# The last batches of a two-layer recurrent and attention kernel: output group 28 two steps earlier, its gated product three steps later

## The chip, the cores and the metric

One core of a Trainium2 chip. The metric is the device time of one execution in microseconds. The kernel before takes 791.45 us (median of three runs, 791.45 to 791.87).

## The reference, cut to what matters

The input x is 16 batches of 256 tokens by 256 features, f32. Layer 0 is a diagonal complex recurrence beside a gated MLP; the change doesn't touch it. Layer 1 is this:

```
xn = layernorm(x)
q = xn @ Wq                      # 16 heads of 192, 64 of them rotated
c_kv, k_rope = split(xn @ Wkv_a) # latents of 64, one shared rotated key of 64
k, v = from rmsnorm(c_kv) @ Wkv_b
scores = q . k / sqrt(192), causal
out = softmax(scores) @ v @ Wo   # 256 x 256 for each batch
g = silu(x @ base_w + b + 2 * lora(top 2 of 8 experts))
x = x + out * g
```

## The kernel before, in words

The key and value weights are folded into the query and output weights ahead of the loop, so that scores and values work on the latents of 64. Every f32 product of projections is done as three fp32r matmuls (high by high, high by low, low by high; helper `three`, line 549).

Layer 1 is a loop over steps n, written out on each engine in the same order; an engine works through its own list and waits for the others on semaphores. Ten steps make a batch: step n computes the scores of unit n. A unit is some rows and heads of a batch, of kind M, W or T. The last batch, 15, has units 150 to 159, by `LAST_ORDER` the W units (whole-width ones) last: 156 to 159.

What happens to a unit n: TensorE makes its scores in step n (`l1_s`, lines 747 to 773), at the earliest when the mask step of unit n-1 has been done and ahead of anything queued later; VectorE adds the mask and takes the row extremes in step n (`most`, line 1589); ScalarE takes the exponentials (`exps`, n+1); VectorE inverts the sums (`inverse`, n+2); GpSimd multiplies (`normalise`, n+2); VectorE turns the weights into PT (`turn_weights`, n+4, before the mask step of n+4 or, in every tenth step, behind it). Two banks take the scores in turn.

What happens to a batch: TensorE multiplies the turned weights by the latents (`l1_pv`, line 795: the value products); the sums lie in four banks. ScalarE copies one half of them to `oh` (`latents`, line 1078, high part), VectorE subtracts this for the low part `ol` (`latents_low`, line 1653). Half k%2 of batch k//2 is output group k: 24 matmuls on TensorE (`l1_out(k)`), then on VectorE the product with the gate (`gated_out(k)`, line 1664, writes `fo[k % 2]`), on GpSimd the addition of x (`residual(k)`, line 2113), and SyncE stores the result. For the last batch the value products come in two pieces: the first at step 160 (needs the turned weights of units 150 to 155), the last at step 162 (needs all ten and the reads of the first piece).

At which step these things stand in each engine's list is set for the last two batches by the table `LAST` (line 178): V the value products, L the reads by ScalarE and VectorE, O the output groups, R the gated product, C the residual; each row has batch 14, then batch 15, and in each the first and second half. Batch 14's two output groups are 28 and 29, those of batch 15 are 30 and 31. In a step of TensorE the order is: value products, scores, output group. In a step of VectorE it is: `latents_low`, `gated_out`, `inverse`, `turn_weights`, `most`. In a step of ScalarE: `latents`, `exps` of the unit before.

Six of the eight banks are a ring (`ring`) that value sums, output groups and others share. `shared_bank_order` (line 142) lists the uses in the order of the steps, use number i has bank `ring[i % 6]`, and `free_shared` makes TensorE wait until the use six places earlier has been read, which for an output group is its gated product:

```
place = jplace[(kind, i)]
if place >= RING:
    for name, value in freed_by(*jorder[place - RING]):
        w.wait_ge(name, value)
...
return {"o": [("ob", i + 1)], ...
```

Of the kernel before, what the change touches and what calls it, by code (L numbers as in the profile page):

```python
# [141 lines left out]
def shared_bank_order():  # L142
# [34 lines left out]

LAST = {
    "V": ((154, 154), (160, 162)),
    "L": ((158, 159), (163, 166)),  # L180
    "O": ((159, 161), (165, 167)),
    "R": ((161, 165), (166, 171)),
    "C": ((164, 165), (168, 173)),
}
LAG = {"V": (LAG_V, LAG_V), "L": (LAG_L, LAG_L), "O": LAG_O, "R": LAG_R, "C": LAG_C}
STEPS = max(LAST["C"][1]) + 1
# [2071 lines left out]
```

How the kernel before makes its waits and increments, by code:

```python
    def wait_ge(self, name, value):  # L99
        if value > self.reached.get(name, 0):
            self.e.wait_ge(self.sems[name], value)
            self.reached[name] = value
# [287 lines left out]
        def after_weights(w):  # L390
            w.wait_ge("wo_t", 4)
            w.wait_ge("wml", 1)
            w.wait_ge("wmh", 1)
# [1 line left out]
        def after_first(w):  # L395
            w.wait_ge("wo_t", 2)
# [1 line left out]
        def after_up(w):  # L398
            w.wait_ge("f1", 8 * NC)
# [1 line left out]
        def after_mlp(w):  # L401
            w.wait_ge("f1", 8 * NC)
            w.wait_ge("f2", 16 * NC)
            w.wait_ge("hsl", 8 * NC)
            w.wait_ge("hsh", 8 * NC)
            w.wait_ge("bu", NC)
# [1 line left out]
        def after_l0(w):  # L408
            after_mlp(w)
            w.wait_ge("xo", 2 * NC)
            w.wait_ge("th0", 2 * NC)
            w.wait_ge("dx", 2 * NC)
            w.wait_ge("ty", 2)
# [1 line left out]
        def qt_free(w, n):  # L415
            if n == 0:
                after_up(w)
            elif n < 3:
                after_mlp(w)
            else:
                w.wait_ge("s", UNITS * ((n - 3) // 2) + HALF_DONE[(n - 3) % 2])
# [10 lines left out]
        def place(e, w, b, h, heads=range(4)):  # L433
            n = 2 * b + h
            w.wait_ge("qq", g_nth[2 * n + 1])
            qt_free(w, n)
            for i in heads:
                for j in range(2):
# [7 lines left out]
        @block.sync  # L447
# [26 lines left out]
                load_x(c)  # L474
            w.wait_ge("w1h", 4)
            w.wait_ge("w1l", 4)
# [22 lines left out]
            def spread(b):  # L500
                w.wait_ge("kvw", b + 1)
                if b == 0:
                    after_mlp(w)
```

## Time and profile before

| | us |
|---|---|
| median of the runs | 791.45 |
| profiled execution | 791.67 |
| its span, first to last instruction | 789.9 |
| TensorE busy | 778.6 |
| VectorE busy | 681.7 |
| ScalarE busy | 524.5 |
| GpSimd busy | 479.5 |

PE is TensorE, DVE VectorE, ACT ScalarE, POOL GpSimd. Times of rows are from the start of the span. A line number in a row is that of the code, and for a matmul of a projection always that of the helper `three`. A row of a timeline can merge several instructions (x2, x24), and its length is then that of all of them. Batch 15's unit 155 is masked by VectorE just before 765.1, 156 in the step that begins at 765.13, and 158 at 770.24. Output group 28 is the run of 24 matmuls that begins at 769.76. The median time from the issue of a store of `fo` to its landing is 2.0 us.

### The profile page before, as it was taken

The page shows a single profiled execution, that of the slowest core. Times are in us where ns is not written, and L with a number is a line of the kernel's source. Part 1 is how long each engine was busy: PE and PEld are TensorE (multiplying, and loading weights), DVE is VectorE, ACT ScalarE, POOL GpSimd, SP SyncE. Part 2 cuts the span into 40 slices and gives each one's busy share as a digit, 9 for nine tenths or more (in the row PEclk, how much of TensorE's full clock was granted, in tenths as well). Part 3 has the DMA queues.
Part 4 walks back from the last instruction along what each step waited for, and adds up shares of the span by engine and source line. Part 5 has one row for each costly group of instructions (what it writes and reads, how often), then busy time and mean ns, then how long its engine had stood idle before and what let it go on. Part 6 is the DMA issues. An engine that isn't in the chain of part 4 may idle for free.

```text
span 789.9 us, 23152 instructions
## 1 busy us (share of the span) xinstructions
PE 778.6 (99%) x7976; PEld 711.5 (90%) x7976; DVE 681.7 (86%) x2616; ACT 524.5 (66%) x1612; POOL 479.5 (61%) x1278
## 2 busy tenths in 40 slices
PE   9999999999999999999999999999999999999988
PEld 7889889888889889898998989899898998989867
DVE  6998897888688899989898998989989898998885
ACT  5554454445555787777767777677777867777682
POOL 6880202202236696776867768686776867768673
PEclk9999999999999999999999999999999999999999
DMA  8600220000002222322222322223222222322220
GB/s 302 253 2 2 62 82 27 1 1 1 1 15 52 40 46 52 61 54 36 48 46 50 64 39 50 40 46 55 56 55 35 48 46 49 63 39 53 34 52 28
DMA packets 101334, 41.15 MB, mean 52 GB/s; under 512 B 91744, under 2 KB 98400, under 8 KB 100576
## 3 DMA queue, kind: packets, MB, share of 16 engines
q1 hardware_dynamic: 98896, 38.89, 22.1%
q8 instruction: 63, 1.03, 0.5%
q10 hardware_dynamic: 2320, 0.79, 0.4%
q14 instruction: 55, 0.45, 0.2%
HBM read 14.47 MB, written 4.19 MB: 24 GB/s over the span
## 4 chain that ended last, share of the span: by engine, by line
PE 92%; DVE 4%; ACT 1%; POOL 1%; issue 1%; ACTq 0%; POOLq 0%; DVEq 0%
PE bank L549 63%; PE bank L773 11%; PE bank L795 8%; PE bank L766 3%; PE bank L629 2%; PE bank L815 1%; PE bank L566 1%; DVE SM L1608 1%; PE bank L681 1%; ACT SM L1065 1%; DVE PT L1631 1%; PE bank L641 1%; PE bank L655 1%; POOL SM L2051 1%; PE bank L700 0%
## 5 line engine op out<-in xcount | busy, mean ns | idle before, releaser
L1065 ACT ACTIVATE SM<-SM,stb 128x224 f32<-128x224 f32 (+7 forms) x512 | 207.2, 407 | 62.7 <-DVE stb L1608 58.2
L2051 POOL TENSOR_SCALAR SM<-SM,stb 128x224 f32<-128x224 f32 (+7 forms) x512 | 195.2, 396 | 67.5 <-DVE stb L1615 66.1
L549 PE MATMUL bank<-yh,wq_lo 128*128 128x256 f32 x512 | 150.6, 294 | 0.0
L549 PE MATMUL bank<-yh,wq_hi 128*128 128x256 f32 x512 | 144.7, 283 | 0.0
L549 PE MATMUL bank<-yl,wq_hi 128*128 128x256 f32 x512 | 144.6, 282 | 0.0
L773 PE MATMUL bank<-KT,QT 128*128 128x192 f32 (+4 forms) x640 | 120.9, 327 | 1.7 <-DVE stb L1608 1.7
L1608 DVE CUSTOM_DVE_ANT_0 SM<-bank,CONST 128x224 f32<-128x224 f32 (+3 forms) x320 | 97.2, 348 | 23.3 <-PE bank L773 20.9
L1631 DVE STREAM_TRANSPOSE PT<-SM 128x128 f32<-128x128 f32 (+2 forms) x232 | 99.7, 462 | 16.7 <-PE bank L795 16.7
L773 PEld LDWEIGHTS bank<-KT,QT 128*128 128x128 f32 x640 | 97.5, 190 | 5.3 <-DVE stb L1608 3.6
L549 PEld LDWEIGHTS bank<-yh,wq_lo 128*128 128x128 f32 x512 | 97.1, 190 | 1.4
L549 PEld LDWEIGHTS bank<-yh,wq_hi 128*128 128x128 f32 x512 | 97.1, 190 | 0.0
L549 PEld LDWEIGHTS bank<-yl,wq_hi 128*128 128x128 f32 x512 | 97.0, 189 | 0.0
L1065 ACT ACTIVATION_READ_ACCUMULATOR SM<-SM,stb 128x1 f32 x512 | 96.9, 189 | 0.0
L950 ACT ACTIVATE hs<-bank,B 128x512 f32<-128x512 f32 x64 | 44.0, 688 | 75.3 <-PE bank L549 70.2
L2044 POOL TENSOR_TENSOR QA<-QA 128x256 f32<-128x256 f32 x62 | 45.9, 740 | 58.7 <-DVE QA L1579 58.7
L1037 ACT ACTIVATE QT<-bank 64x512 f32<-64x512 f32 x128 | 75.6, 590 | 6.5 <-PE bank L549 5.0
L1579 DVE TENSOR_TENSOR QA<-bank,TR 128x512 f32<-128x512 f32 x124 | 79.4, 683 | 0.1
L549 PE MATMUL bank<-woe_hi,ol 128*128 128x256 f32 x256 | 75.4, 294 | 0.7 <-issue 0.7
L549 PE MATMUL bank<-w2h,hl 128*128 128x256 f32 x256 | 74.0, 289 | 0.2 <-DVE w2l L1352 0.2
L549 PE MATMUL bank<-w2h,hh 128*128 128x256 f32 x256 | 72.4, 283 | 0.0
L549 PE MATMUL bank<-w2l,hh 128*128 128x256 f32 x256 | 72.3, 283 | 0.0
L549 PE MATMUL bank<-woe_hi,oh 128*128 128x256 f32 x256 | 72.1, 281 | 0.0
(229 smaller groups left out, 2068.9 us busy)
## 6 DMA issues: line engine op xcount, KB each, us to landing
QT<-QA SPq DMA_DIRECT2D x240, 64.0 KB, 2.1
PT<-KV SPq DMA_DIRECT2D x256, 16.0 KB, 1.8
out<-fo SPq DMA_DIRECT2D x32, 128.0 KB, 2.0
X<-in_x SPq DMA_DIRECT2D x7, 512.0 KB, 11.5
stage<-in_wqn SPq DMA_DIRECT2D x2, 1024.0 KB, 5.3
stage<-in_wo SPq DMA_DIRECT2D x2, 1024.0 KB, 4.9
stage<-in_w1t SPq DMA_DIRECT2D x4, 256.0 KB, 5.0
stage<-in_w2t SPq DMA_DIRECT2D x2, 512.0 KB, 6.2
```

The lines of the kernel that those rows point to most:

```text
L549: i = e.matmul(dst, a, b, start=(first and j == 0), stop=(last and j == 2), skip_group_check=skip)
L766: j = e.matmul(sbank[n % 2][32 * i:32 * i + 32, at:to], KT[b % 3][:, p, 32 * kb:32 * kb + 32], Q[:, :, kb:3, i, :], start=True, stop=True)
L773: j = e.matmul(sbank[n % 2][:, at], Q[:, q, :, :].rearrange("p h c -> p (h c)"), KT[b % 3][:, p, 0:32 * q + 32], start=True, stop=True)
L795: j = e.matmul(sums[64 * half:64 * half + 64, :, 32 * q:32 * end], C[rows_, kb // 2, at], PT[rows_, 2 * half:2 * half + 2, kb, q:end, :], ...
L950: e.activation(hs[g % 2][:, :], fbank[g % 2][:, :], ACT.Gelu, bias=B1[:, g % 8:g % 8 + 1]).then_inc(SEM["gelu"], 1)
L1037: i = e.activation(QT[r, (2 * b + g // 2) % 3, p, :, g % 2:4:2, :].rearrange("p n j c -> p j n c"), src[r, :, :, :], ACT.Copy)
L1065: i = e.activation(M[:, at], M[:, at], ACT.Exp, bias=S[:, 0, j:j + 1], scale=-1.0, accum_out=S[:, 1, j:j + 1])
L1579: i = e.tensor_tensor(A[:, part, :, :, g % 2, :], src, TR[:, part, :].rearrange("p (n c) -> p n c", n=8).unsqueeze(1).broadcast_to([128, 2 ...
L1608: i = e.tensor_tensor_reduce(M[:, at], bk[:, at], mask[:, 224 - 32 * q:256], 1.0, 3e38, ALU.add, ALU.min, S[:, 0, j:j + 1])
L1631: return e.transpose(PT[:, slot, 0:k, q:q + some, :].rearrange("p k q c -> p q k c"), src)
L2044: e.tensor_tensor(A[:, 0, 0, :, :], A[:, 0, 0, :, :], A[:, 1, 1, :, :], ALU.subtract)
L2051: i = e.tensor_scalar(P[:, at], P[:, at], S[:, 2, j:j + 1], 1.0, ALU.mult, ALU.mult)
```

## The change

Four rows of the table `LAST` get other steps for batch 14. ScalarE and VectorE read the first half of its sums in step 156 instead of 158. Output group 28 is issued in step 157, behind the scores of unit 157, instead of in step 159 behind those of unit 159. Its gated product is in VectorE's step 164 instead of 161, which is behind the turn of unit 159 (step 163). The residuals of groups 28 and 29, and with them their stores, stand one step later each.

```diff
 LAST = {
     "V": ((154, 154), (160, 162)),
-    "L": ((158, 159), (163, 166)),
-    "O": ((159, 161), (165, 167)),
-    "R": ((161, 165), (166, 171)),
-    "C": ((164, 165), (168, 173)),
+    "L": ((156, 159), (163, 166)),
+    "O": ((157, 161), (165, 167)),
+    "R": ((164, 165), (166, 171)),
+    "C": ((165, 166), (168, 173)),
 }
```

## Rows read from the trace of the kernel before

**Rows 1.** The page, part 4: share of the span on the chain, by engine.
```profile
PE 92%; DVE 4%; ACT 1%; POOL 1%; issue 1%; ACTq 0%; POOLq 0%; DVEq 0%
```

**Rows 2.** Busy time of each engine in three stretches of the tail, us from the start.
```profile
762.50:770.00 7.50, 5.45 (x38) 3.81 (x26) 6.98 (x40) 6.91 (x31) 4.80 (x16) 1.00 0.18 50
770.00:775.60 5.60, 5.48 (x121) 4.71 (x121) 5.46 (x21) 2.90 (x10) 3.21 (x8) 1.00 0.00 0
775.60:789.90 14.30, 10.81 (x200) 10.40 (x200) 4.92 (x9) 2.18 (x4) 3.13 (x5) 0.97 0.12 39
```

**Rows 3.** The chain that ended last, from 772 us: start, length in us.
```profile
772.14 0.77 DVE PT L1631 x2
...
772.96 2.60 PE bank L795 x92
775.56 3.04 PE bank L549 x24
778.60 1.92 PE bank L795 x117
```

**Rows 4.** Timeline of VectorE: start, length in us, idle before in brackets.
```profile
765.13 0.19 DVE L1615 RECIPROCAL stb<-stb 128x6 f32<-128x6 f32 x1
...
768.37 1.29 DVE L1653 TENSOR_TENSOR ol<-bank,oh 128x512 fp32r<-128x512 f32 x2 [0.46 <-ACT oh L1078]
769.57 0.16 DVE L1615 RECIPROCAL stb<-stb 128x2 f32<-128x2 f32 x1
...
770.24 0.36 DVE L1608 CUSTOM_DVE_ANT_0 SM<-bank,CONST 128x224 f32<-128x224 f32 x1
...
773.52 0.70 DVE L1631 STREAM_TRANSPOSE PT<-SM 128x512 f32<-128x512 f32 x1
774.14 0.40 DVE L1664 SCALAR_TENSOR_TENSOR fo<-bank,PT 128x256 f32<-128x256 f32 x1
...
774.76 1.28 DVE L1631 STREAM_TRANSPOSE PT<-SM 128x512 f32<-128x512 f32 x2
776.31 1.29 DVE L1653 TENSOR_TENSOR ol<-bank,oh 128x512 fp32r<-128x512 f32 x2 [0.27 <-ACT oh L1078]
777.52 0.70 DVE L1631 STREAM_TRANSPOSE PT<-SM 128x512 f32<-128x512 f32 x1
```

**Rows 5.** Timeline of ScalarE, the same columns.
```profile
764.91 0.19 ACT L1065 ACTIVATION_READ_ACCUMULATOR SM<-SM,stb 128x1 f32 x1
...
767.74 1.09 ACT L1078 ACTIVATE oh<-bank 128x512 fp32r<-128x512 f32 x2
...
773.57 0.49 ACT L1065 ACTIVATE SM<-SM,stb 128x224 f32<-128x224 f32 x1 [1.50 <-DVE stb L1608]
...
775.61 1.09 ACT L1078 ACTIVATE oh<-bank 128x512 fp32r<-128x512 f32 x2 [0.96 <-PE bank L795]
```

**Rows 6.** Timeline of TensorE, the same columns.
```profile
762.58 1.90 PE L773 MATMUL bank<-KT,QT 128*128 128x128 f32 x10
765.13 1.08 PE L773 MATMUL bank<-KT,QT 128*128 128x224 f32 x4 [0.65 <-DVE stb L1608]
766.66 1.08 PE L773 MATMUL bank<-KT,QT 128*128 128x224 f32 x4 [0.46 <-DVE stb L1608]
...
769.76 0.36 PE L549 MATMUL bank<-woe_hi,ol 128*128 128x256 f32 x1 [0.71 <-issue]
```

**Rows 7.** Timeline of GpSimd, the same columns.
```profile
763.81 4.62 POOL L2051 TENSOR_SCALAR SM<-SM,stb 128x32 f32<-128x32 f32 x15 [1.66 <-DVE stb L1615]
...
775.81 0.74 POOL L2113 TENSOR_TENSOR fo<-fo,X 128x256 f32<-128x256 f32 x1
```

**Rows 8.** Busy times and granted clock after TensorE's last matmul.
```profile
786.40:788.00 1.60, 0.01 (x1) 0.00 (x0) 0.42 (x1) 0.00 (x0) 0.72 (x1) 1.00 0.00 0
788.00:789.00 1.00, 0.00 (x0) 0.00 (x0) 0.00 (x0) 0.00 (x0) 0.00 (x0) 0.97 0.38 130
789.00:789.90 0.90, 0.00 (x0) 0.00 (x0) 0.00 (x0) 0.00 (x0) 0.00 (x0) 0.50 0.01 1
```

## The prediction

> **What bounds the kernel now.** First the chain that ended last, by engine: TensorE holds 92% of it, VectorE 4% [rows 1]. Over the whole span the kernel is TensorE's, but the change touches only the last 30 us or so, and those have to be read by themselves. The busy times in three stretches show it [rows 2]: from 762.5 to 770.0 us TensorE is busy for 5.45 of 7.50 us and VectorE for 6.98; from 770.0 to 775.6 both are nearly full; from 775.6 on TensorE leads with 10.81 us of work and VectorE has 4.92. The chain, followed through the hand-over, says where the lead changes [rows 3]: VectorE's last turn of a non-W unit (unit 155) ends at 772.91, TensorE's first value products of batch 15 start at 772.96, then come without a pause output group 29 (775.56, 3.04 us) and the last value products (778.60). So everything up to 772.9 is set by VectorE, and everything behind it by TensorE's queue. The profiled execution took 791.67 us, 0.22 above the median of 791.45; its span is 789.9 and the 1.77 us around it are taken as they are.
>
> **What is moved, step by step.** No instruction is added or removed. I write O28 for output group 28, and G28 for its gated product.
>
> 1. *Reads of batch 14's first half, step 158 to 156 (ScalarE and VectorE).* In their old place they cost VectorE a wait of 0.46 us for ScalarE and 1.29 us of work, starting 0.63 us after ScalarE's copy [rows 4, 5]: VectorE was through with step 157 at 768.37 - 0.46 = 767.91. In the new place ScalarE can start them only when the exponentials of unit 154 are out, about 765.11, since they stand behind these in its queue; the first step of VectorE behind unit 155 starts 0.63 later, at 765.74, instead of 765.13. The sums that they read were complete long before (TensorE began the next unit's scores at 762.58 [rows 6]). The two subtractions end at 767.03, and the next instruction, which before began 1.20 after the first subtraction (769.57 - 768.37), starts at 766.94. Steps 156 and 157 then take VectorE 2.78 us as before (765.13 to 767.91), to 769.72.
> 2. *O28, step 159 to 157 (TensorE).* TensorE began it 0.10 us after the subtractions (769.66 to 769.76), so now at 767.13, behind the scores of unit 157, which still start at 765.13 and take 1.08 [rows 6]. It takes 3.04 us, the length of its twin O29 in the chain [rows 3]. Now the scores of units 158 and 159 are queued behind it. Those of 158 run from 770.17 to 771.25 instead of from 766.66. VectorE, free at 769.72, has a reciprocal and a turn to do first, 0.67 us by the old distance from 769.57 to 770.24, and would take these scores at 770.4: it waits until 771.29, 0.04 behind their end. That is 1.05 us later than the old 770.24 [rows 4]. The scores of 159 follow directly and are done by about 772.3, before VectorE asks for them at 773.9. GpSimd is no limit: its multiplications run at 4.62 us for 15 [rows 7], the six of unit 154 would be done about 769.1, and they are wanted at 769.7.
> 3. *Up to the first value products.* From the mask step of 158 VectorE runs as before: second half's subtractions, reciprocal, turn of 155. The end of that turn, and with it the start of the value products, comes 1.05 later: 774.01 instead of 772.96. So the 2.05 us in which TensorE idled in the first stretch [rows 2] are only partly filled and partly moved behind the scores of 159.
> 4. *G28, VectorE's step 161 to 164, and what waits for it.* This is the step that decides. The shared banks are a ring of six, handed out in the order that `shared_bank_order` writes. Counting it out, O28 is place 308, then one pad, four banks for batch 15's sums, and O29 is place 314: six further, the same bank. `free_shared` therefore makes TensorE wait, ahead of O29 and of all that is queued behind it, for G28. Before, G28 ended at 774.54 and O29 could start at 775.56, so the wait cost nothing. The move puts G28 behind the subtractions of group 30 (step 163) and behind the turn of unit 159 in VectorE's queue. The subtractions of group 30 need the first value products complete. The chain becomes: value products 774.01 to 776.61 (2.60); ScalarE's copies 0.05 later; VectorE's subtractions 0.70 after these start, as before (775.61 to 776.31), at 777.36; the last turn 1.21 further (776.31 to 777.52), at 778.57; G28 another 0.62 further (as 773.52 to 774.14 behind such a turn) at 779.19, 0.40 long [rows 4, 5]; O29 0.10 behind it, at 779.69. Before it was at 775.56. TensorE stands still from 776.61 to 779.69, 3.1 us, where it had none.
> 5. *Who would have hidden it.* O29 was the cover for VectorE's tail: its 3.04 us ran beside the subtractions and the last turn, which ended at 778.22, just before the last value products at 778.60. Now O29 comes after that tail, and the tail's wait is in the open. The last value products themselves find their operands ready. The turns of 157 and 158 are no nearer limit: exponentials of 159 shift by 1.05 with the mask step, from 773.57 to 774.62, and release the turns 1.19 later (774.76 before), at 775.8; 1.28 us of turns end at 777.1, before 777.36 [rows 4, 5].
> 6. *The residual and the store of 28.* They follow G28, some 5 us later than before. G30, in the same output buffer, waits for that store; G28 ends at 779.6, 0.74 us of GpSimd [rows 7] and some 2 us of transfer bring it to about 782.5, and G30 can't come before O30, which stands behind O29 and the last value products, is done (about 787). Nothing. Steps 165 and 166 of the copies on GpSimd hold up nothing either: its multiplications end with step 161. SyncE's queue holds at that time only the stores.
>
> The sum: +1.05 (VectorE's wait for the scores of 158) and +3.1 (O29 behind G28) is 4.15 us; everything behind O29 keeps its order and lengths. 791.67 + 4.15 = 795.8 for the profiled execution, 795.6 on the median's footing.
>
> Bounds of what the trace doesn't show. The wait of O29 has no row. From below it would be nothing or a gain, if VectorE reached G28 before 776; from above it is the 3.1 us and a TensorE that runs slower after them. I take 3.1, since each of its parts is the distance between two rows of this tail. The shift of 1.05 lies between -0.46 (only ScalarE's old wait gone) and 3.04 (VectorE held for the whole of O28); I take 1.05, since it comes from the starts of both engines' next work, and both have rows.
>
> The clock: the granted clock is 1.00 in the first two stretches, and the third's 0.97 comes from its very end [rows 2]. After TensorE's last matmul (786.4) it is 1.00 to 788, 0.97 in the next microsecond and 0.50 at the end [rows 8], so it fell to the lower of its levels (1.2 GHz for 2.4) after some 2.5 us without work. The pause in front of O29 would be 3.1 us.
> The Trainium skill ("TensorE: Matmul & The Clock Gate", section "Why this matters for your kernels") warns of just such pauses between bursts of matmuls, since idleness puts the array back to half rate; by that rule O29 would run at the lower level at least in part, while by the sum above it doesn't. The page and these rows speak the same way, so this is a rival with a real chance.
>
> **The rivals.**
>
> *A. The clock falls in the new pause.* For it: it fell after about 2.5 us at the end. Against it: that was one fall, and in the first stretch TensorE idled for 2.05 of 7.50 us in pieces without one. O29's 3.04 us would take up to 3.04 us more if all of it ran at 0.50; the clock should rise again on the way, so I take half, 1.5: 797.1.
>
> *B. Faster: the holes are filled and nothing new opens.* The place is O29's start. If G28 is through before 776 (another bank for O29, or VectorE early), O29 follows the value products directly; with TensorE's 2.05 us of idle time of the first stretch all gained, 789.4. It decides by whether VectorE's queue or TensorE's brings O29's bank. Against it: the ring's count, and that G28 stands behind the subtractions which themselves need the value products.
>
> *C. Only the ring's wait.* VectorE isn't held up by the scores of 158 (O28 shorter or the queue less strict than I have it), only step 4 costs: 3.1, 794.6.
>
> *D. No effect.* The wait exists, but TensorE's other work covers it: 791.5. Against it: only the last value products are left behind it, and they are queued after O29.
>
> **The numbers.** Forecast 0.50, A 0.33, C 0.10, D 0.03, B 0.04. The likeliest is 795.6, its own range 795.0 to 796.3. For 8 in 10 the range takes in A with half of its scatter and most of C: 794.0 to 798.0; B, D and a full loss of the clock are outside. A change of 0.2% (1.6 us) either way is about what a measurement here can tell from no change. Slower by more than that: forecast, A and C, 0.93; same 0.03; faster 0.04.
>
> **What would show it.** Step 2: O28 starts near 767.1, behind the scores of 157, and VectorE waits some 0.9 us for the scores of 158. Step 3: value products start near 774.0. Step 4: a pause of TensorE of 3 us in front of O29, released by VectorE's G28. Step 5: the last value products follow O29 at once. A: granted clock below 1 in the rows of 779 to 783, O29 longer than 3.04. I am wrong if O29 starts before G28, if there is no such pause, or if the value products start before 773.

## The result and the profile after

The changed kernel takes 797.54 us (median of five runs, 797.25 to 798.42), the kernel before 791.45 in the same comparison: a ratio of 1.0077 (95% interval 1.0066 to 1.0088), 6.1 us slower. The profiled execution took 798.28 us with a span of 796.4.

The code up to the tail is the same, but the time that it takes is not: over all profiles of this study the mark that I measure tails from, the start of the scores of unit 155 (the first row of [rows 6]), lies between 762.08 and 763.26. From there on the profiles of one kernel repeat: e3_early and e10_early_look are the same program, and the way from the mark to the end of the span is 28.17 and 28.16 us. Before, the mark is at 762.58 and the span ends 27.32 us later; here it is at 762.46, and the end comes 33.94 us later. The tail is 6.62 us longer.

The chain that ended last, after (answers to [rows 3]):

```profile
772.96 0.68 DVE PT L1631 x2
...
773.68 2.63 PE bank L795 x92
...
776.34 0.61 ACT oh L1078
...
777.07 0.43 DVE ol L1653
...
778.36 0.62 DVE PT L1631
778.97 0.32 DVE fo L1664
...
779.34 5.49 PE bank L549 x24
784.82 2.26 PE bank L795 x121
787.09 3.06 PE bank L549 x24
```

Read it downwards. VectorE turns unit 155, the first value products run, ScalarE copies their sums, VectorE subtracts, turns unit 159 and then makes the gated product of group 28 (`fo`); only when that is out does TensorE start group 29, at 779.34. Before, the third piece of this chain was already group 29, straight behind the value products. And group 29 now takes 5.49 us where it took 3.04, the last value products 2.26 where they took 1.92.

TensorE's timeline (answers to [rows 6]):

```profile
762.46 1.90 PE L773 MATMUL bank<-KT,QT 128*128 128x128 f32 x10
765.00 1.08 PE L773 MATMUL bank<-KT,QT 128*128 128x224 f32 x4 [0.64 <-DVE stb L1608]
767.01 0.36 PE L549 MATMUL bank<-woe_hi,ol 128*128 128x256 f32 x1 [0.93 <-ACT oh L1078]
...
769.94 1.78 PE L773 MATMUL bank<-KT,QT 128*128 128x224 f32 x8
773.68 2.61 PE L795 MATMUL bank<-PT 32*64 32x384 f32 x96 [1.97 <-DVE PT L1631]
779.34 0.58 PE L549 MATMUL bank<-woe_hi,ol 128*128 128x256 f32 x1 [3.05 <-DVE fo L1664]
```

Group 28 is now the run from 767.01. The scores of 158 and 159 (769.94, eight matmuls) come behind it. Two pauses stand in brackets: 1.97 us ahead of the value products, 3.05 us ahead of group 29.

VectorE's timeline (answers to [rows 4]):

```profile
765.62 1.29 DVE L1653 TENSOR_TENSOR ol<-bank,oh 128x512 fp32r<-128x512 f32 x2 [0.67 <-ACT oh L1078]
...
770.95 0.39 DVE L1608 CUSTOM_DVE_ANT_0 SM<-bank,CONST 128x224 f32<-128x224 f32 x1 [0.68 <-PE bank L773]
...
777.07 1.29 DVE L1653 TENSOR_TENSOR ol<-bank,oh 128x512 fp32r<-128x512 f32 x2 [0.30 <-ACT oh L1078]
778.27 0.70 DVE L1631 STREAM_TRANSPOSE PT<-SM 128x512 f32<-128x512 f32 x1
778.90 0.39 DVE L1664 SCALAR_TENSOR_TENSOR fo<-bank,PT 128x256 f32<-128x256 f32 x1
```

The subtractions of group 28 wait 0.67 us for ScalarE, the mask step of 158 waits 0.68 us for the scores that stand behind group 28, and the gated product follows the last turn at once.

Busy times and granted clock around the long pause (TensorE's busy time is the first figure behind the length, the granted clock the third from the end):

```profile
777.00:778.00 1.00, 0.00 (x0) 0.00 (x0) 0.93 (x2) 0.42 (x1) 0.00 (x0) 1.00 0.00 0
778.00:779.00 1.00, 0.00 (x0) 0.00 (x0) 1.00 (x3) 0.00 (x0) 0.00 (x0) 0.83 0.00 0
779.00:780.00 1.00, 0.66 (x3) 0.67 (x4) 0.28 (x1) 0.00 (x0) 0.63 (x1) 0.50 0.00 0
...
785.00:786.00 1.00, 1.00 (x61) 1.00 (x58) 0.29 (x1) 0.00 (x0) 0.63 (x1) 0.76 0.00 0
```

The clock goes from 1.00 to 0.50 in the microsecond from 778, while TensorE still waits, and is back in the microsecond from 785. At 0.50 a matmul of group 29 starts every 0.213 us instead of every 0.119.

From the mark, the value products start 11.22 us later against 10.38 before: 0.84. The pause adds 3.05. The slow clock adds 2.45 (5.49 - 3.04) and 0.34 (2.26 - 1.92). Together 6.7, against the 6.62 measured.

### The profile page after: what moved, and what is told of

It is laid out like the page before. It is cut to its first block, busy times and chain, and to the rows that moved or that the text cites. A ratio compares the mean times of both kernels' runs of the same rounds, so it can differ in the third digit from the quotient of the medians.

```text
span 796.4 us, 23151 instructions
## 1 busy us (share of the span) xinstructions
PE 780.8 (98%) x7976; PEld 714.2 (90%) x7976; DVE 681.1 (86%) x2616; ACT 522.9 (66%) x1612; POOL 478.7 (60%) x1278
## 4 chain that ended last, share of the span: by engine, by line
PE 92%; DVE 3%; ACT 1%; POOL 1%; issue 1%; ACTq 0%; POOLq 0%; DVEq 0%
PE bank L549 63%; PE bank L773 11%; PE bank L795 8%; PE bank L766 3%; PE bank L629 2%; PE bank L815 1%; PE bank L566 1%; DVE SM L1608 1%; PE bank L681 1%; ACT SM L1065 1%; DVE PT L1631 1%; PE bank L641 1%; PE bank L655 1%; POOL SM L2051 1%; PE bank L700 0%
## 5 line engine op out<-in xcount | busy, mean ns | idle before, releaser
L549 PE MATMUL bank<-woe_lo,oh 128*128 128x256 f32 x256 | 73.0, 285 | 0.0
```

The lines of the kernel that those rows point to most:

```text
L549: i = e.matmul(dst, a, b, start=(first and j == 0), stop=(last and j == 2), skip_group_check=skip)
```

## The experiments

The kernel before ran beside the experiments, in four groups with medians of 791.64, 791.61, 791.53 and 791.58 us, and in none of those 67 runs was the mean granted clock below 0.999. Tails are counted from the mark as above, minus the 27.32 us of before.

**Another bank for group 29 (e1_banks).** In the changed kernel:

```diff
+    i, j = js.index(("o", 2 * NB - 3)), js.index(("o", 2 * NB - 2))
+    js[i], js[j] = js[j], js[i]
     return js
```

> The changed kernel, with the ring places of output groups 29 and 30 exchanged, so that group 29 has a bank that nobody has to free and group 30 gets the bank of group 28. Theory (the bank's wait and the clock that falls in its pause make nearly all of the loss): the pause of 3.05 us before group 29 is gone, the granted clock stays 1.00 to the end of the matmuls, value products still start about 0.8 us late, so about 792.2 us. Rival 1 (the late gated product costs by itself, on VectorE or by the late store): at least 795 us although group 29 starts on time. Rival 2 (the clock falls because of the other holes, before the value products): clock still at 0.50 somewhere behind 774 us, about 794 to 795 us. Rival 3 (B of the prediction, the filled holes are a gain): 789.4 us.

Median 793.25 us (8 runs), ratio 1.0021 (1.0011 to 1.0031), tail +0.82. Its chain around group 29:

```profile
774.47 2.61 PE bank L797 x92
777.08 3.05 PE bank L551 x24
780.12 1.92 PE bank L797 x118
```

Group 29 starts the moment the value products end (774.47 + 2.61 = 777.08) and takes 3.05. With the late gated product still in step 164, nearly all of the loss has gone: its lateness costs nothing by itself, what costs is that it holds the bank. The median is 1 us above what I expected. Part of that is the clock, as the runs of e3_early show below; but the five runs at full clock, too, have a median of 793.12. The profiled one of them (793.20) is late before the tail begins: its mark is at 763.26, 0.68 us behind that of the kernel before. What makes that time differ is not shown.

**Only the gated product late (e2_product).** In the kernel before:

```diff
-    "R": ((161, 165), (166, 171)),
-    "C": ((164, 165), (168, 173)),
+    "R": ((164, 165), (166, 171)),
+    "C": ((165, 166), (168, 173)),
```

> The kernel before with only the gated product of group 28 moved from step 161 to 164 and the residuals of 28 and 29 to 165 and 166; reads and output group 28 stay in steps 158 and 159. Theory: group 29 waits for its bank for about 3.05 us, the clock falls in that pause and costs 1.7 to 2.8 us more, value products start on time at about 773.0: 796.2 to 797.3 us. Rival (it takes both halves of the change, because group 28's early place makes the holes in which the clock falls): the wait only, clock 1.00, 794.5 us. Rival 1 of the first run would give the same loss with group 29 on time.

Median 797.02 us, ratio 1.007 (1.0056 to 1.0084); all five runs have a mean clock of 0.995 to 0.998. In its profile the tail is +4.55: a pause of 3.05 us, and group 29 at 4.54 us. This half of the change alone makes 5.4 of the 6.1 us, the clock's part included.

**Only the reads and group 28 early (e3_early).** In the kernel before:

```diff
-    "L": ((158, 159), (163, 166)),
-    "O": ((159, 161), (165, 167)),
+    "L": ((156, 159), (163, 166)),
+    "O": ((157, 161), (165, 167)),
```

> The kernel before with only the reads of batch 14's first half moved to step 156 and output group 28 to 157; gated product and residuals stay where they were. Theory: VectorE waits about 0.7 us for ScalarE and 0.7 us for the scores of unit 158, in place of its old 0.46 us, value products start about 0.8 us late, no wait for the bank, clock 1.00: 792.2 us, the same as e1_banks within 0.3. Rival 3 (filled holes are a gain): 789.4 to 790 us. Rival (the shift is caught up later): 791.5 us.

Median 793.21 us (9 runs), ratio 1.0021 (1.0011 to 1.0031); tail +0.85 in the profile, with a clock of 1.00 from the mark to the last matmul. So moving group 28 into TensorE's idle time is a loss of 0.85 us, not a gain: VectorE gets the scores of 158 late. The runs are in two groups. Five, with a mean clock of 0.999 or more, took 792.47 to 793.21 us; four, with 0.997 or 0.998, took 793.85 to 795.22. e1_banks has the same two groups, five at 792.37 to 793.31 and three at 793.97 to 794.99. The median of e3_early's five is 792.49, 0.85 us above the kernel before, as in the tail.

**The long pause filled (e4_filled).** In the changed kernel, 18 matmuls ahead of group 29's wait, whose sums are overwritten:

```diff
+                        if 2 * d + qt == 2 * NB - 3:
+                            w.wait_ge("oth", evacuated(d, 1))
+                            w.wait_ge("otl", evacuated(d, 1))
+                            w.wait_ge("ob", 2 * NB - 5)
+                            for c in range(6):
+                                three(jof("o", 2 * NB - 2)[:, 0:256], oh[1][:, c % 8, :], ol[1][:, c % 8, :],
+                                      woe_hi[:, c % 8, :], woe_lo[:, c % 8, :], True, True)
                         l1_out(2 * d + qt)
```

> The changed kernel, with 18 further matmuls of group 29's own kind (128x256, 0.12 us each, 2.2 us in all; their sums are overwritten later and reach no result) on TensorE in the pause before group 29; the wait for the bank stays. Theory (two costs that stand in a row, wait and clock): the clock stays 1.00, group 29 still starts when the gated product is done and takes 3.04 us: 795.2 us, that is 2.3 us less than the changed kernel. Rival (the matmuls of group 29 are slow for another reason, as sharing memory with VectorE or the store): group 29 still takes about 5.5 us and the time stays at 797.5 us.

```profile
774.13 2.63 PE bank L795 x92
...
779.42 0.32 DVE fo L1671
...
779.78 3.15 PE bank L549 x24
```

```profile
779.78 0.39 PE L549 MATMUL bank<-woe_hi,ol 128*128 128x256 f32 x1 [0.72 <-DVE fo L1671]
```

```profile
779.00:780.00 1.00, 0.28 (x2) 0.22 (x2) 0.73 (x2) 0.00 (x0) 0.19 (x1) 1.00 0.00 0
```

The added matmuls leave 0.72 us of the pause idle, and the granted clock stays 1.00. Group 29 still waits for the gated product (779.42 to 779.74) and then takes 3.15 us instead of 5.49. The tail is +3.98 us, beside the 4.15 of my sum, which left the clock out. So wait and clock are two costs in a row, and the slow matmuls were the clock's doing. The median is 796.59 (ratio 1.0063, 1.005 to 1.0075), 1.4 above what I expected. Two of the five runs have a mean clock of 0.998 (797.05 and 797.61). Neither has a profile; the 1.97 us pause ahead of the value products, which is not filled here, may be the cause, but that is not shown. The three at 0.999 or more took 796.00 to 796.59, so the clock is not all of it: in the profiled one (796.00) the mark is 0.32 us later than before, and the rest is open.

**The gated product in step 163 (e5_step163).** In the changed kernel, ahead of the last turn:

```diff
-    "R": ((164, 165), (166, 171)),
+    "R": ((163, 165), (166, 171)),
```

> The changed kernel with the gated product of group 28 one step earlier on VectorE: step 163, behind the subtractions of group 30, ahead of the turn of unit 159. Theory (pause plus clock): the product starts 0.62 us earlier and group 29 with it, the pause is 2.4 us instead of 3.05. If the clock falls by then as it did in the changed kernel (some 2.3 us into the pause), it falls here too and the time is 0.6 us below that of the changed kernel; if this pause is short enough for the clock to stay, 2.3 to 3.3 us below, about 794.6 us. Rival (only a place behind all of VectorE's turns costs): as e3_early, 792.5 us.

```profile
774.00 2.63 PE bank L795 x92
...
778.67 0.34 DVE fo L1664
...
779.05 4.62 PE bank L549 x24
```

```profile
779.05 0.42 PE L549 MATMUL bank<-woe_hi,ol 128*128 128x256 f32 x1 [2.45 <-DVE fo L1664]
```

The pause is 2.45 us, 0.60 shorter, and the clock falls all the same, after group 29 has begun (0.63 in the microsecond from 779, then 0.50): 4.62 us. Its tail is +4.80, beside +5.45 in the second profile of the changed kernel (the next run). The median is 797.63 (ratio 1.0071, 1.0058 to 1.0083), not told from the changed kernel's: from run to run these times differ by more than the 0.6 us that the shorter wait gives back.

**The changed kernel once more (e7_again).**

> The changed kernel itself once more, beside the others on the same chip, for a second profile of its pause. Theory: pause 3.05 us, clock at 0.50 somewhere from 778 us on, cost of the clock between 1.5 and 2.8 us from run to run, median near 797.5 us. Rival (the fallen clock of the first profile was a rare event): clock 1.00, near 795.6 us.

Median 797.07 us (796.96 to 799.37), ratio 1.0074 (1.0061 to 1.0086). The two pieces of its chain and its clock:

```profile
779.40 4.54 PE bank L549 x24
783.94 1.98 PE bank L795 x119
```

```profile
779.00:780.00 1.00, 0.60 (x5) 0.60 (x6) 0.35 (x2) 0.00 (x0) 0.57 (x1) 1.00 0.00 0
780.00:781.00 1.00, 1.00 (x10) 1.00 (x9) 0.00 (x0) 0.00 (x0) 0.16 (x1) 0.81 0.00 0
783.00:784.00 1.00, 1.00 (x13) 0.78 (x20) 0.02 (x1) 0.00 (x0) 0.00 (x0) 0.50 0.00 0
784.00:785.00 1.00, 1.00 (x74) 1.00 (x81) 0.40 (x1) 0.00 (x0) 0.52 (x1) 0.99 0.00 0
```

The same pause, but the clock falls 1.2 us or so after TensorE has resumed, and it is back at about 784. Here it costs 1.50 and 0.06 us where the first profile had 2.45 and 0.34. All ten runs of the changed kernel had a mean clock of 0.995 to 0.998.

**The shorter pause: filled, and profiled again (e8_hole_filled, e10_early_look, e11_early_look).** e8 is e3_early with 12 matmuls ahead of the value products, whose sums are overwritten; the other two are e3_early unchanged, one run each:

```diff
+                if n == 160:
+                    w.wait_ge("ob", 2 * NB - 5)
+                    for c in range(4):
+                        three(jof("o", 2 * NB - 2)[:, 0:256], oh[0][:, c, :], ol[0][:, c, :],
+                              woe_hi[:, c, :], woe_lo[:, c, :], True, True)
```

> e3_early with 12 further matmuls (1.45 us, their sums reach no result) on TensorE behind the scores of unit 159, in the pause of 1.97 us before the first value products. The runs of e3_early and e1_banks lie in two groups: those whose mean granted clock is 0.999 to 1.0 at 792.4 to 793.3 us, those with 0.997 or 0.998 at 793.9 to 795.2. Theory (in those the clock fell in or behind this shorter pause): with the pause filled all runs keep 0.999 or more, and the median is 792.5 us with no run above 793.4. Rival (the scatter comes from another place): medians and scatter as e3_early, 793.2 us, some runs at 0.997.

> e3_early once more for a profile. Theory: if this run is one of those with a mean clock below 0.999 (4 of 9 had it), its rows show a granted clock of 0.50 that begins at or behind the pause before the first value products, some 772 to 776 us, and the time is 1.4 to 2.7 us longer; else it is as e3_early's profile. Rival: the clock falls somewhere else, or is 1.00 in a long run.

> As e10_early_look, for a further chance to see one of the runs with the lower mean clock; the same expectations.

e8: median 792.45 us, 11 runs from 792.25 to 793.07, every clock 0.999 or 1.0; ratio 1.0012 (1.0003 to 1.0021). The upper group is gone, though in the profile 0.54 us of the pause stays idle. e8 ran on another chip than e3_early, e10 and e11 on the same chip as e8. e10 had a clock of 1.00 and took 792.75 us. e11 was one of the others (mean 0.998, 793.57 us):

```profile
773.31 3.74 PE bank L795 x96
777.05 3.44 PE bank L549 x24
```

```profile
772.00:773.00 1.00, 0.00 (x0) 0.00 (x0) 1.00 (x4) 0.41 (x2) 0.32 (x1) 1.00 0.00 0
773.00:774.00 1.00, 0.69 (x16) 0.42 (x24) 1.00 (x7) 0.08 (x1) 0.59 (x2) 1.00 0.00 0
774.00:775.00 1.00, 1.00 (x32) 0.69 (x24) 0.88 (x2) 0.99 (x4) 0.91 (x2) 0.73 0.00 0
775.00:776.00 1.00, 1.00 (x32) 0.86 (x24) 0.98 (x3) 0.00 (x0) 0.72 (x2) 0.50 0.00 0
...
777.00:778.00 1.00, 1.00 (x9) 1.00 (x6) 0.20 (x1) 0.90 (x2) 0.00 (x0) 0.56 0.28 92
```

The pause of 1.97 us ends at 773.31; the clock falls in the microsecond from 774, with TensorE busy again, and is back in the one from 777. The value products take 3.74 us instead of 2.60 and group 29 3.44 instead of 3.05: 1.5 us.

**VectorE unloaded (e6_weigh, e9_unloaded, e12_ahead).** If VectorE bounds all up to the first value products [rows 2, 3], what nobody waits for should leave that stretch. e6 moves the gate's product of batch 15 from step 154 to 165:

```diff
-                if n and (d := sum_of(n - 1)) is not None:
+                if n and (d := sum_of(n - 1)) is not None and d < NB - 1:
                     weigh(d)
+                if n == 165:
+                    weigh(NB - 1)
```

> The kernel before with one thing moved that the change left where it is: the product of the gate of batch 15 (VectorE, 0.58 us on the chain at step 154, not wanted until group 30's gated product in step 166) goes to step 165, where VectorE has an idle time of 2.2 us. Theory (up to 772.96 us VectorE is the bound and TensorE behind it): the first value products start 0.4 to 0.6 us earlier and all behind them follows, about 0.5 us less than before. Rival (TensorE's value products of batch 14 or ScalarE's exponentials hold that stretch): no change within 0.1 us.

Median 791.64 us beside 791.61, ratio 0.9998 (0.9989 to 1.0007): no difference told. In its profile the value products start 0.33 us earlier from the mark, and the tail is -0.31. That is about half of the 0.58 us that left, because the rival is in part right: VectorE now waits 0.33 us at 762.61 for TensorE's value products of batch 14, where before it waited for nothing. The rest is lost in the scatter of the times.

e9 has this edit of e6 and moves more:

```diff
-LAST_LORA, LAST_SUM, LAST_SPREAD = 152, 153, 149
+LAST_LORA, LAST_SUM, LAST_SPREAD = 152, 161, 149
+    i = js.index(("o", 2 * NB - 4))
+    js[i], js[i + 1] = ("pad", i), js[i]
-    "R": ((161, 165), (166, 171)),
-    "C": ((164, 165), (168, 173)),
+    "R": ((164, 165), (166, 171)),
+    "C": ((165, 166), (168, 173)),
```

> The kernel before with VectorE's work that nobody waits for taken out of its bound stretch: the sum of the gate of batch 15 goes from step 153 to 161, its product from 154 to 165, the gated product of group 28 from 161 to 164 (with its residual as in the change), and group 28 and the pad behind it exchange places in the ring, so that group 29 has the bank of the gate's sum and not that of group 28. Reads and output group 28 stay at 158 and 159. Theory (VectorE bounds everything up to the first value products): these start up to 1.2 us earlier, no pause before group 29, clock 1.00: 790.4 to 791.0 us, below the kernel before. Rival 1 (ScalarE or TensorE take over as the bound at once): 791.4 us. Rival 2 (the sum in step 161 delays the subtractions of group 30 and the last value products): value products early, last ones late, 791.5 to 792 us.

Median 792.04 us, ratio 1.0007 (0.9999 to 1.0016), tail +0.37: both rivals at once. VectorE first waits 0.91 us for TensorE at 762.6, since the turn of unit 150 needs batch 14's value products out of the way, and so the two steps ahead of the mark yield little. Then the chain shows this:

```profile
775.05 0.59 DVE PT L1558
...
775.66 0.02 ACT w1b L1061
...
776.20 0.59 ACT oh L1080
```

The gate's sum (L1558) keeps ScalarE's tanh (L1061) back until 775.66, and the copies of the first value products, queued behind it, start at 776.20 though those were done by 775.2. Group 29 had a pause after all: it now has the bank of the gate's sum, and waits 0.52 us for it (775.16 to 775.68).

e12 is e6 with ScalarE's copies of batch 14's first half a step earlier than their subtractions:

```diff
+                    if n == 157 and qt == 0:
+                        latents(NB - 2, 0)
-                    if (d := due("L", n, qt)) is not None:
+                    if n != 158 and (d := due("L", n, qt)) is not None:
```

> The kernel before with the gate's product of batch 15 at step 165 (as e6_weigh) and ScalarE's copies of batch 14's first half one step earlier than VectorE's subtractions of them: ScalarE copies in step 157, between the exponentials of 155 and those of 156, VectorE subtracts in 158 as before. Theory (VectorE bounds from 762.6 to 772.96 us, and its one wait there is the 0.46 us for these copies): the wait goes, the value products start 0.46 us earlier than in e6_weigh and 0.8 us earlier than before, no pause of TensorE is longer than before, clock 1.00: about 790.7 us. Rival (the exponentials of 156, now behind the copies, are late for VectorE's reciprocal): no gain over e6_weigh, 791.3 us.

```profile
771.30 0.76 DVE PT L1633 x2
...
772.10 2.61 PE bank L795 x92
774.71 3.05 PE bank L549 x24
```

The value products start at 772.10, 9.62 us behind the mark (762.48) where it was 10.38: 0.76 earlier, and the rest follows without a pause. In e6 they start 10.05 us behind the mark, so the last 0.43 came with the copies: VectorE still waited 0.33 us for them in e6 and doesn't here. Median 790.88 us (790.69 to 791.79, 11 runs) beside 791.58; ratio 0.9992 (0.9983 to 1.0001). The medians are 0.7 us apart and the start of the value products says 0.76, but the interval still takes in 1. It has the lowest median of this study, and for its gain one profile speaks, not the interval.

## Why the prediction was right, and which of its terms was off

The range (794.0 to 798.0) holds the time, the direction was right, and what happened is my forecast with rival A on top of it. The likeliest number, 795.6, and its own range (795.0 to 796.3) were missed: the time, 797.54, is near A's 797.1, which I had given 0.33.

1. *Step 1, the reads.* Right: the wait for ScalarE is 0.67 us, from 764.95 to 765.62; I had 0.61.
2. *Step 2, group 28.* Right in kind: VectorE waits 0.68 us for the scores of 158. I had 0.9, having counted 3.04 us of group 28 and 1.08 of scores in full; from the start of group 28 to the end of the scores of 158 it is 3.91 us, since their matmuls overlap. (The description of the kernel says that a unit's scores wait for the mask step of the unit before. In the code, `w.wait_ge("mx", n - 1)` in `l1_s`, it is the unit two before, since two banks take the scores in turn: the scores of 158 started at 766.66, right behind the mask step of 156. The step was worked out from the rows and isn't changed by this.)
3. *Step 3.* The value products are 0.84 us late (I said 1.05); e3_early alone gives 0.85.
4. *Step 4, the bank.* Right: the pause is 3.05 us (I said 3.1), released by the gated product. e1_banks takes it away and e2_product makes it alone.
5. *Steps 5 and 6.* Right: the last value products follow group 29 at once, and the store of 28 delays nothing.
6. *The clock is the term that was mis-sized.* My sum had it at nothing and rival A at 1.5 us with a chance of 0.33. The two profiles of the changed kernel give 2.8 and 1.6 us, and all ten runs had the lower mean clock, as had all of e2_product and e5_step163. Sum and clock make 795.6 + 1.6 to 2.8 = 797.2 to 798.4; the ten runs lie between 796.96 and 799.37, four of them above the upper end of my range. What misled me is an argument that I made against A: that 2.05 us of idle time in the first stretch had not brought the clock down. That idle time was in four pieces (0.65, 0.46, 0.23 and 0.71 us); it says nothing of a pause in one piece. The evidence for A (a fall some 2.5 us after the last matmul [rows 8]) was the row that was alike, and I should have made A the forecast.
7. *What I had not seen at all:* the shorter pause ahead of the value products, 1.97 us, which the early group 28 opens, also brings the clock down in part of the runs: e11_early_look shows it in a profile, and by the mean clock it is seven of seventeen in e1_banks and e3_early. For e3_early this is why the median lies 0.7 us above the tail; for e1_banks it is so only in part, since its runs at full clock are late as well.

The rule of the Trainium skill ("TensorE: Matmul & The Clock Gate", section "Why this matters for your kernels"), that long pauses between bursts put the array back to half rate, holds here: in each of the three profiles with the pause of 3.05 us unfilled (the changed kernel twice, e2_product) the clock went to 0.50 in it or right behind it, and in those of e4_filled and e8_hole_filled, whose pauses are filled for the most part, it stayed at 1.00.

C and D are refuted (the tail without the clock is +3.98 in e4_filled, not 3.1 or 0). So is B: with the bank free, e1_banks is still slower than before, because the holes of TensorE lay in a stretch that VectorE bounds, and a hole that is filled there only comes up again later and in one piece.

## What to carry to other kernels

Before you move the reader of a shared buffer back, count out who gets that buffer next: the cost is not the reader's lateness but the next owner's wait with everything queued behind it. Work moved into idle time of an engine that isn't the bound gained nothing here, and lost 0.85 us because the bound engine's inputs were queued behind it. A pause of TensorE of two or three microseconds in one piece had a second price behind it, the clock, and that price changed from run to run; so look for it in every run's mean clock and not in one profile.

## What the runs showed of the hardware

The granted clock can fall after the pause is over: in e7_again in the microsecond from 780, with group 29 running since 779.40, in e11_early_look in the one from 774, with TensorE busy since 773.31. In the two profiles of the changed kernel the clock's part behind the same pause was 1.6 and 2.8 us. The time at 0.50 was about 3.4 us in e7_again and about 6.8 in the first profile of the changed kernel. All 20 runs with an unfilled pause of 3.05 or 2.45 us ahead of group 29 (the changed kernel's ten, five each of e2_product and e5_step163) had a mean clock of 0.993 to 0.998, and in the four of them with a profile it fell in that pause or within 1.3 us behind it. Fifteen of these also have the pause of 1.97 us, so for the long pause alone the five of e2_product speak. With only the pause of 1.97 us (e1_banks, e3_early and its two further profiles) 8 of 19 runs had 0.997 or 0.998. In the tail of the kernel before, whose pauses ahead of the last matmul are at most 0.71 us, none of the 67 runs was below 0.999.
